# Which chunk runs the one remaining turn of edges in a four-layer graph network

## The reference

```python
edge_index = jnp.stack([src, dst])
x = _layernorm(x + _L0_gnn_ref(x, edge_index, edge_weight, ...))      # gcn
x = _layernorm(x + _L1_gnn_ref(x, edge_index, edge_type_8, ...))      # ggnn, 2 steps
x = _layernorm(x + _L2_gnn_ref(x, edge_index, L2_gnn_W, ...))         # gat
x = _layernorm(x + _L3_gnn_ref(x, edge_index, edge_attr_64, ...))     # mpnn
# inside each layer: gather rows by src, weigh them, sum them by dst
msgs = h[src_f] * norm[:, None]
out = jax.ops.segment_sum(msgs, dst_f, num_segments=N)
```

## Time and profile before

| what | value |
|---|---|
| median of three runs | 10787.64 us (10786.82 to 10789.09) |
| the profiled execution | 10789.09 us |
| its span, first to last instruction | 10787.3 us |
| mean granted PE clock | 0.728 of full speed |
| busy share of the span | PE 56%, DVE 49%, POOL 45%, ACT 14% |

### The profile page before, as it was taken

One profiled execution on the slowest core, in us unless ns is written; L12 is line 12 of the kernel. 1 busy time (PEld: TensorE's weight loads), 2 busy tenths in 40 slices (PEclk: granted clock), 3 DMA queues, 4 the chain that ended last, 5 costly groups with the idle time before them and its releaser, 6 DMA issues. The chain is left out here.

```text
span 10787.3 us, 166167 instructions
## 1 busy us (share of the span) xinstructions
PE 6086.2 (56%) x60710; PEld 5248.2 (49%) x60711; DVE 5239.6 (49%) x7210; ACT 1520.2 (14%) x4256; POOL 4871.8 (45%) x5701
## 2 busy tenths in 40 slices
PE   4666659997433334443333333586999635545554
PEld 3333339995233333323333333486999634444444
DVE  7888878885211111121122222597888743323333
ACT  3666640001100000000000000132000001101101
POOL 2111110001577777757777777001000147777775
PEclk7777779998666666666666666555999867767776
DMA  1000032223222122221111111475322112222222
GB/s 46 0 0 0 0 46 83 83 83 118 79 66 66 53 66 66 66 72 53 52 52 52 52 52 52 163 292 190 112 93 92 63 54 79 79 80 79 73 79 73
DMA packets 322858, 798.38 MB, mean 74 GB/s; under 512 B 157570, under 2 KB 196012, under 8 KB 303436
## 3 DMA queue, kind: packets, MB, share of 16 engines
q1 hardware_dynamic: 147804, 423.30, 11.6%
q0 software_dynamic: 153216, 312.49, 10.2%
q10 hardware_dynamic: 21744, 61.34, 1.4%
HBM read 714.98 MB, written 81.79 MB: 74 GB/s over the span
## 5 line engine op out<-in xcount | busy, mean ns | idle before, releaser
L984 POOL DMA_INDIRECT ggnn_edges_G<-trans_d,ggnn_edges_rid x3136 | 2975.5, 949 | 1199.3 <-issue 955.1
L1097 PE MATMUL ggnn_edges_PS<-ggnn_edges_OH,ggnn_edges_G 128*128 128x128 f32 x6272 | 1176.8, 373 | 2317.1 <-DMA ggnn_edges_G<-trans_d,ggnn_edges_rid 2207.2
L1097 PEld LDWEIGHTS ggnn_edges_PS<-ggnn_edges_OH,ggnn_edges_G 128*128 128x128 f32 x6272 | 1136.7, 285 | 2361.7 <-issue 2360.2
L984 POOL DMA_INDIRECT mpnn_edges_G<-msg_d,mpnn_edges_rid x1568 | 1499.8, 956 | 659.5 <-issue 473.0
L1053 DVE TENSOR_TENSOR acc<-acc,ggnn_edges_PS 128x128 f32 x224 | 64.6, 288 | 2510.7 <-PE ggnn_edges_PS L1097 2510.7
L1081 PE MATMUL mpnn_edges_PS<-wt_late,mpnn_edges_at 128*128 128x256 f32 x1568 | 545.3, 522 | 682.1 <-DVE mpnn_edges_G L1040 339.9
L620 ACT ACTIVATE prep_OJF<-prep_OJ,prep_fld 128x98 bf16<-128x98 bf16 x3136 | 848.9, 362 | 555.0 <-DVE prep_OJ L676 555.0
L1081 PEld LDWEIGHTS mpnn_edges_PS<-wt_late,mpnn_edges_at 128*128 128x128 f32 x1568 | 414.8, 272 | 794.1 <-DVE mpnn_edges_G L1040 361.1
L826 PE MATMUL prep_PS<-prep_OJF,prep_OHr 128*128 128x490 bf16 x1582 | 580.7, 549 | 211.5 <-DVE prep_OHr L705 211.5
L1040 DVE TENSOR_TENSOR mpnn_edges_G<-mpnn_edges_G,mpnn_edges_PS 128x1792 f32<-128x1792 f32 x112 | 226.3, 2020 | 878.9 <-DMA mpnn_edges_G<-msg_d,mpnn_edges_rid 702.0
L1018 DVE SCALAR_TENSOR_TENSOR ggnn_edges_OH<-dstI,ggnn_edges_itm,ggnn_edges_PS 128x896 f32<-128x896 f32 x448 | 491.6, 1144 | 228.7 <-issue 164.1
(11 more groups left out here) (454 smaller groups left out, 10933.6 us busy)
## 6 DMA issues: line engine op xcount, KB each, us to landing
ba_rows<-slot_d SPq DMA_DIRECT2D x49, 3136.0 KB, 11.4
HB<-slot_d SPq DMA_DIRECT2D x49, 1568.0 KB, 6.3
heads_rows<-slot_d SPq DMA_DIRECT2D x49, 1568.0 KB, 6.3
ggnn_edges_G<-trans_d,ggnn_edges_rid POOLq DMA_INDIRECT x3136, 2.5
mpnn_edges_at<-in_edge_attr SPq DMA_DIRECT2D x112, 448.0 KB, 3.6
trans_d<-gcn_edges_tb ACTq DMA_DIRECT2D x49, 512.0 KB, 2.7
trans_d<-ggnn_edges_tb ACTq DMA_DIRECT2D x49, 512.0 KB, 3.0
mpnn_edges_G<-msg_d,mpnn_edges_rid POOLq DMA_INDIRECT x1568, 2.5
```

The source lines that it names most:

```text
L984: pool.indirect_dma_start(G[:, s, c, :], None, table, bass.IndirectOffsetOnAxis(ap=rid[:, s, c:c + 1].bitcast(U32), axis=0)).then_inc(gath ...
L1097: mm = pe.matmul(wp[s % 2], G[:, s, c, :], OH[:, s % 2, c, :], start=c == 0, stop=c == GC - 1)
```

## The change

The table of the leftover passes is computed in another way. With t an entry of `turns_to` and f the flag, the old table is 2 t f, with its last entry raised to at least 1. The new one is (2 t - 1) f + 1, with its entry 0 set to 0. With f = 1 both are 2 t, since entry 0 of `turns_to` is 0. With f = 0 the old table is 0, 0, 0, 0, 0, 0, 0, 1 and the new one 0, 1, 1, 1, 1, 1, 1, 1.

```diff
                     own.step(V.tensor_scalar(flag[:], over_all, 0.0, None, ALU.is_gt))
-                    own.step(V.tensor_scalar(tmore[:], turns_to[:, 0:NCH + 1], float(SL // FS), None, ALU.mult))
-                    own.step(V.tensor_scalar(tmore[:], tmore[:], flag[:, 0:1], None, ALU.mult))
-                    own.step(V.tensor_scalar(tmore[:, NCH:], tmore[:, NCH:], 1.0, None, ALU.max))
+                    own.step(V.tensor_scalar(tmore[:], turns_to[:, 0:NCH + 1], float(SL // FS), -1.0, ALU.mult, ALU.add))
+                    own.step(V.tensor_scalar(tmore[:], tmore[:], flag[:, 0:1], 1.0, ALU.mult, ALU.add))
                     own.step(V.tensor_copy(turns_o[:], tmore[:]))
+                    own.step(V.memset(turns_o[:, 0:1], 0))
```

## The result

| | before | changed |
|---|---|---|
| median of four runs each, us | 10787.23 (10783.31 to 10789.09) | 10851.69 (10847.27 to 10852.40) |
| the profiled execution, us | 10789.09 | 10841.94 |
| its span, us | 10787.3 | 10840.2 |

The ratio is 1.0057, with a 95% interval of 1.0045 to 1.0070: 64.5 us slower at the medians, where 58.0 were forecast. The spans of the two profiled executions differ by 52.9 us only.

What follows compares the result with a forecast made beforehand. Chunk 0 would wait for the turn's 28 gathers, with nothing else in hand: gcn 43.3 - 15.7 = +27.6, gat 45.3 - 14.9 = +30.4, together +58.0 on 10787.64, giving 10845.6 us, range 10835 to 10857.

Steps and rivals of the forecast that it cites:

- The table's own instructions: In `prep`: a cast moves up and a maximum becomes a fill, hidden by SP's stores; put at 0.
- What is removed: Ahead of chunk 6: the turn's computing goes away, 15.7 us in gcn and 14.9 in gat, 30.6 in all.
- What is added, first term: Ahead of chunk 0: from first gather to start of the 28th, 34.3 us, with ends 33.7 and 36.7.
- a mean duration under 1000 ns: Both stages: expected sign that the gathers average under 1000 ns each and take about 34 us.
- Terms 2 to 4: Chunk 0: 28th gather to PE's products 2.62 us (gat +2.1); third, to DVE's add, 6.4; then to ACT's copy 1.89.
- The delays: Chunk 0's copy comes later by 43.3 us in gcn (41.4 to 45.7) and 45.3 in gat (43.3 to 47.8).
- what is left over: Freed overlap in chunks 0 and 1, and PE's recent work at chunks 0 and 6: put at 0, within 1 us.
- That the whole delay is paid: Chunk 0, both stages: no other work is in hand, so all of its delay (43.3 and 45.3 us) counts.
- The clock rival: Chunk 1: PE stays at the low clock after idling, +9 to +19 us, about 10855 to 10865; chance 0.05.
- the cheaper gathers: Front of both stages: gathers land sooner, first term 25 to 30 us, total 10828 to 10837; chance 0.04.
- not slower: Chunk 0's delay is below chunk 6's gain of 15.7 and 14.9 us; 10757 if all hidden; chance 0.03.
- No other stage changes: Outside gcn_edges (28 us longer) and gat_edges (30), no stage changes by more than a few us.

Runs made afterwards that it cites:

- e3: Kernel before, with the leftover turn moved from ahead of chunk 6 to ahead of chunk 2 in both stages; 10789.04 us, ratio 1.0000.
- e4: Kernel before, with a second table so DVE and PE skip the turn while SP and POOL still run its loads and gathers; 10758.83 us, ratio 0.9973.
- e7: Changed kernel with DVE's one-hot and weights product run three times per item in gcn_edges; 12550.01 us on another chip (kernel before there 12503.86).
- e5: Changed kernel with DVE's one-hot and weights product left out of gcn_edges; 12561.61 us on another chip (kernel before there 12503.86).
- e2: Kernel before, with the leftover turn moved from ahead of chunk 6 to ahead of chunk 1 in both stages; 10809.86 us, ratio 1.0021.
- e1: Kernel before, with the turn moved ahead of chunk 0 in gcn_edges only, gat_edges keeping it ahead of chunk 6; 10817.91 us, ratio 1.0028.
- e6: Changed kernel with that gcn_edges product's second operand read from PSUM, equally long; 12565.22 us on another chip (kernel before there 12503.86).

## Why the prediction was right

The forecast was 10845.6 us, +58.0. The two stages show +59.3; the median, 10851.69, is within the range of 10835 to 10857, but its +64.5 is 0.5 us above the forecast's own 53 to 64. The mechanism is the one forecast. That the sum came within 1.3 us is in part luck: gcn cost 29.65 for 27.6 and gat 29.65 for 30.4, so that 0.75 of gcn's 2.05 us was made up by an error the other way. By its steps:

- *The table's own instructions*: 0, and the stages outside the two differ only as executions do. e3, whose table takes as many instructions as that of before, is at 1.0000. What the changed table itself costs is not measured by itself.
- *What is removed*: 15.7 and 14.9 us were put down to chunk 6 from the even steps. Shown by e4: skipping the turn there gives 15.0 and 14.5 in the stages, 29.9 in all at the medians, for the 30.6; most of what is missing is the 0.6 and 0.2 us behind chunk 6's copy, where e4 has waits of its own.
- *What is added, first term*: undersized in gcn. The 28 gathers take 37.3 us for the 34.3 taken, 0.6 more than the upper end of 36.7. The prediction saw that DVE's operations lengthen gathers, from a 1.72 us one, which was 0.78 longer than the usual 0.94 beside an operation of 1.09 us. But the 0.6 us that it added for "one or two" is less than even one of these, and the products of the turn are twice as long: the two cost 1.6 and 1.8 us. e7 shows that each product lengthens one gather, and e5 that without them the term is 33.9. The sign that named this, a mean duration under 1000 ns, failed in gcn (1072 ns). In gat the term was right, 34.5 us, though partly by how things fell: one product started 0.12 us after a gather (8575.35 after 8575.23), which stayed at 0.94 us, and the next gather took 1.71; the other product comes behind the last gather. In e2 the same product meets a gather earlier on and makes it 2.69 us.
- *Terms 2 to 4*: 2.69, 6.18 and 1.79 us in gcn for 2.62, 6.4 and 1.89. The next stage's items were a good stand-in. In gat they are 4.57, 5.62 and 1.78 us, for 4.72, 6.4 and 1.89; the third term was 0.8 us shorter than taken, which is most of the error in gat's delay.
- *The delays*: chunk 0's copy is late by 46.1 us in gcn (43.3 forecast, upper end 45.7) and by 46.45 - 2.01 = 44.4 in gat (45.3). With chunk 6's gain and some tenths along the stage and at its end (0.7 us in gcn, about nothing in gat; the prediction put 0 for what is left over) they come to 29.65 each, for 27.6 and 30.4.
- *That the whole delay is paid*: shown by e2 and e3, which move nothing but the turn. e2's chunk 1 pays only for the time by which it is due before the gathers are through, and e3's chunk 2, due after them, pays nothing.
- *The clock rival*: the steps from chunk to chunk didn't grow, 26.05 for 26.08 us, and chunk 1 follows chunk 0 after 17.64 us (2604.97 to 2622.61), for 17.65 of before. PE was granted a mean of 0.83 of full speed in 2622:2635, the first 13 us of chunk 1, and 0.96 in the next 13 (2635:2648), where before had 0.83 in 2583:2596 and 0.95 in 2596:2609. So the clock didn't stay down.
- *The rivals of the cheaper gathers and of "not slower"*: the gathers took 34.5 and 37.3 us, never less than the undisturbed 33.7.
- *"No other stage changes"*: the prediction called itself wrong if another stage changed by more than a few us, and the first stretch is 6.6 us shorter in the profiled execution. It is put down above to the spread between executions, as the first stretch differs by up to 5.4 us among e1 to e4; a small effect of the change on it isn't excluded.

## What to carry to other kernels

Work that waits for a slow transfer should stand where the transfer has landed; later than that gained nothing here. Against the last position, ahead of chunk 6, the turn cost +59 us ahead of chunk 0, +21 ahead of chunk 1 and 0 ahead of chunk 2, and the place where the cost ends can be estimated from two rows, the last gather and the due time of a chunk. The turn that is run only because the loop needs one was better skipped by the engines on the path (-30 us here), while the engines off it kept it. The distance between even steps was a good measure of what a step with extra work costs: in each stage it was within 0.7 us of what taking the work out gave back.

## What the runs showed of the hardware

A gather that POOL starts while a DVE TENSOR_TENSOR with both operands in SBUF is under way is lengthened until 0.8 to 0.9 us after that operation's end: 2.55 and 2.72 us for 0.94, beside operations of 2.02 us. With one operand in PSUM (e6) the gathers have a mean of 0.95 us. A gather that had started 0.12 us before such an operation (in `gat_edges` of the changed kernel) wasn't lengthened, nor was one of before that started 0.01 us into it (2574.12, L316 at 2574.11); one that started 0.09 us into it was (L317 above). The Trainium skill, "SBUF — State Buffer", section "Who interferes with whom", infers that a `tensor_tensor` would not stall the building of descriptors; the runs show that it holds up these indirect DMAs, by up to 1.8 us here. That the operands, and not the length, decide is in line with what the same section says of DVE's second SBUF input, that it gets in the way of a GpSimd instruction that reads SBUF; no run here shows what part of a gather's issue is such a read.

On the second chip the kernel before took 12503.86 us, 16% more, and e5 shows where at least a part of it lies: from the first index load of one ggnn stage to that of the next it takes 5331.86 - 2803.19 = 2528.7 us, for 4798.34 - 2778.31 = 2020.0 in the trace of before. It isn't the gathers: they still take 0.94 us and start 1.25 apart within an item. In that stretch of before, PE waits 1107.0 us for the gathers of L1097's products; in e5 it waits 48.4 us for them, and 1121.8 us in which the profile names nothing that it waited for. Its timeline shows these as gaps of mostly 2.43 us between single matmuls of 0.37 us, within one item. DVE's add waits for them, and POOL then waits for DVE's next indices, 685.6 us for 186.2 in before. In `gcn_edges` there are no such gaps, and its chunks stand 26.0 us apart as on the first chip. Why PE is slow to go on there stays open.
